# FFN first parts: two of the four pair copies of groups 0 to 6 made by VectorE instead of ScalarE

## The reference

```
xn = layernorm(x)
z = layernorm(xn) * ln1_g + ln1_b
q, v = z @ wq.T + bq, z @ wv.T + bv ; k = q
attn = softmax(q k.T / 4) @ v, 16 heads ; a = attn @ w_out.T + b_out
h = gelu(xn @ ternary(W1).T + b1)            # (4096, 1024)
f = h @ ternary(W2).T + b2
return x + a + f
```

## Time and profile before

| what | value |
|---|---|
| median of 3 runs | 1436.72 us (1434.46 to 1441.07) |
| profiled execution: time, span | 1435.52 us, 1433.7 us |
| busy share of the span: PE, DVE, ACT, POOL | 97%, 93%, 87%, 8% |
| VectorE share of the chain that ended last | 71% (the maxima of line 839: 68%) |
| first parts on ScalarE (line 1020) | 32, mean 1148 ns |
| second parts on VectorE (line 831) | 32, mean 1282 ns |

### The profile page before, as it was taken

How to read it: one execution, slowest core, us unless ns; L and a number is a source line. 1 busy time by engine, 2 the same in 40 slices (tenths; PEclk the granted TensorE clock), 3 DMA queues, 4 the chain that set the end, 5 groups by cost and what they waited for, 6 DMA issues and landing times.

```text
span 1433.7 us, 32248 instructions
## 1 busy us (share of the span) xinstructions
PE 1384.6 (97%) x13414; PEld 447.5 (31%) x13414; DVE 1339.1 (93%) x1430; ACT 1247.3 (87%) x2284; POOL 113.7 (8%) x246
## 2 busy tenths in 40 slices
PE   7899987999999999999999999999999999999999
PEld 5666542222222222222222222222222222222244
DVE  7868779999999999999999999999999999999934
ACT  5554643999999999999999999899999999999975
POOL 2000005000000000000000000000222200002200
PEclk8999999999999999999999999999999999999999
DMA  6012000010000000100000001001212101001122
GB/s 232 16 36 76 30 16 1 28 31 30 31 31 31 30 31 30 31 30 26 29 30 29 32 29 33 28 32 35 60 61 61 61 31 33 32 33 60 39 100 81
DMA packets 28531, 60.69 MB, mean 42 GB/s; under 512 B 6200, under 2 KB 11736, under 8 KB 28130
## 3 DMA queue, kind: packets, MB, share of 16 engines
q1 hardware_dynamic: 27810, 56.99, 11.8%
q10 hardware_dynamic: 576, 1.65, 0.3%
HBM read 41.29 MB, written 16.77 MB: 40 GB/s over the span
## 4 chain that ended last, share of the span: by engine, by line
DVE 71%; PE 23%; ACT 2%; DMA 2%; issue 1%; POOL 0%; SPq 0%; ACTq 0%; DVEq 0%
DVE part_max L839 68%; PE ps L367 6%; PE ps L384 3%; PE ps L1070 3%; PE ps L1139 3%; PE ps L330 2%; PE ps L1085 2%; PE ps L458 1%; DVE w L831 1%; ACT w L1020 1%; DMA rows<-in_rows 1%; PE ps L439 1%; ACT hidden L1015 1%; PE ps L1111 1%; ACT w L1049 1%
## 5 line engine op out<-in xcount | busy, mean ns | idle before, releaser
L1049 ACT ACTIVATE w<-ps 128x512 f32<-128x512 f32 x2048 | 1111.4, 596 | 63.8 <-PE ps L384 21.6
L839 DVE TENSOR_REDUCE part_max<-ps 128x1 f32<-128x1024 f32 x1024 | 1164.8, 1211 | 1.9 <-PE ps L330 1.7
L367 PE MATMUL ps<-w,v_ones 128*32 128x256 f32 (+1 forms) x7688 | 628.6, 399 | 0.4
L384 PE MATMUL ps<-qry,key 50*128 50x512 f16 x1984 | 411.4, 388 | 7.2 <-ACT w L1049 7.0
L330 PE MATMUL ps<-qry,key 48*128 48x512 f16 x2048 | 404.2, 380 | 11.4 <-DVE part_max L839 11.3
L367 PEld LDWEIGHTS ps<-w,v_ones 128*32 128x32 f32 x7688 | 152.2, 108 | 384.7 <-issue 211.5
L384 PEld LDWEIGHTS ps<-qry,key 50*128 50x128 f16 x1984 | 101.1, 93 | 440.7 <-ACT w L1049 412.5
L330 PEld LDWEIGHTS ps<-qry,key 48*128 48x128 f16 x2048 | 101.5, 95 | 36.8 <-DVE part_max L839 26.4
L638 POOL COPY v_ones<-v_all 128x128 f32<-128x128 f32 x64 | 18.6, 291 | 743.9 <-PE ps L367 743.9
L1011 ACT ACTIVATE q_split<-ps,sigma_bq 128x512 f16<-128x512 f32 x16 | 11.0, 687 | 65.2 <-PE ps L1085 65.2
L1070 PE MATMUL ps<-w_ternary,w 128*128 128x256 f16 x512 | 61.7, 277 | 6.2 <-DVE w L831 6.2
(11 more groups left out here) (144 smaller groups left out, 466.2 us busy)
## 6 DMA issues: line engine op xcount, KB each, us to landing
key<-q_parts SPq DMA_DIRECT2D x64, 128.0 KB
qry<-q_parts SPq DMA_DIRECT2D x64, 128.0 KB
o_heads<-o_evacuated SPq DMA_DIRECT2D x31, 256.0 KB, 10.2
resid<-in_x SPq DMA_DIRECT2D x8, 512.0 KB, 13.8
q_parts<-q_split SPq DMA_DIRECT2D x16, 256.0 KB, 2.5
key<-q_parts SPq DMA_DIRECT2D x64, 64.0 KB
qry<-q_parts SPq DMA_DIRECT2D x64, 64.0 KB
out<-resid SPq DMA_DIRECT2D x7, 512.0 KB, 3.1
```

What stands on the lines that cost most here:

```text
L367: mm = eng.matmul(pv[32 * c:32 * c + 2 * D, c0:c1], vst[:, kb, :], prob[kb % 2][:, c * BANK + c0:c * BANK + c1], start=(kb == 0), stop=(kb ...
L384: eng.matmul(ring_bank(v, i, False), key[v][r:r + KROWS, kb * P:(kb + 1) * P], qry[v][r:r + KROWS, c * BANK:(c + 1) * BANK], start=True, s ...
L839: dve.tensor_reduce(part_max[h % 2][:, a // 2, a % 2:a % 2 + 1], pa[a % 2], AX.X, ALU.max).then_inc(s_r, 1)
L1049: act.activation(prob[kb % 2][:, c * BANK:(c + 1) * BANK], ring_bank(k, i, last), ACT.Exp, scale=exp_scale).then_inc(s_e, 1)
```

## The change

In groups 0 to 6 the first parts of pairs 1 and 3 are written by VectorE, with a tensor_scalar (`hidden` times the scale, float16 out) right ahead of the second part of the same pair. It waits for the gelu of the pair's second block, and the second part waits for it through a new semaphore. ScalarE keeps pairs 0 and 2 of these groups and all four of group 7; its counter's values are counted anew. 14 instructions move, none is added in number. TensorE's stream is the same.

```diff
--- before.py
+++ after.py
@@ -266,6 +266,7 @@
         s_h = sem("hidden_psum")
         s_g = sem("gelu_done")
         s_h1 = sem("hidden_part1")
+        s_hd = sem("hidden_part1_dve")
         s_h2 = sem("hidden_part2")
         s_f = sem("ffn_psum")
         s_ra = sem("resid_ffn_added")
@@ -310,6 +311,20 @@
 
 
         BETWEEN = (1, 3, 5)
+
+        def on_dve(g, i):
+
+            return g < NG - 1 and i % 2 == 1
+
+        ACT_PAIRS = [[i for i in range(KF // 2) if not on_dve(g, i)] for g in range(NG)]
+
+        def act_parts(g, i):
+
+            return sum(len(a) for a in ACT_PAIRS[:g]) + sum(1 for n in ACT_PAIRS[g] if n <= i)
+
+        def dve_parts(g, i):
+
+            return KF // 2 * g + i + 1 - act_parts(g, i)
         EARLY = 6
 
 
@@ -825,7 +840,13 @@
                         rows(2 if g == NG - 1 else 1)
                     if i == KF // 2 - 1:
                         value(g, 0)
-                    dve.wait_ge(s_h1, KF // 2 * g + i + 1)
+                    if on_dve(g, i):
+                        dve.wait_ge(s_g, KF * g + 2 * i + 2)
+                        dve.tensor_scalar(hp[0][:, 2 * i:2 * i + 2, :], hid[:, 2 * i:2 * i + 2, :], hs[:, 0:1], None,
+                                          ALU.mult).then_inc(s_hd, 1)
+                        dve.wait_ge(s_hd, dve_parts(g, i))
+                    else:
+                        dve.wait_ge(s_h1, act_parts(g, i))
                     if g == 0 and i == 0:
                         dve.wait_ge(s_wd, 8)
                     dve.scalar_tensor_tensor(out=hp[1][:, 2 * i:2 * i + 2, :], in0=hid[:, 2 * i:2 * i + 2, :],
@@ -1013,7 +1034,7 @@
                 for f in range(KF):
                     act.wait_ge(s_h, KF * g + f + 1)
                     act.activation(hid[:, f, :], pf[f % 2], ACT.Gelu, scale=1.0 / XS, bias=b1_col[:, f:f + 1]).then_inc(s_g, 1)
-                    if f % 2:
+                    if f % 2 and not on_dve(g, f // 2):
                         if first and f == 1:
                             act.wait_ge(s_wd, 4)
                         act.wait_ge(s_g, KF * g + f + 1)
```

## The result

The changed kernel takes 1440.15 us (median of 12 runs, 1437.78 to 1442.92) against 1435.19 us before (12 runs, 1433.56 to 1441.07). The ratio is 1.0025 with a 95% interval of 1.0014 to 1.0037, which is 3.6 us (2.0 to 5.3) at 1436 us. The two medians lie 4.96 us apart, the two means 3.8; I go by the ratio. The forecast was 1439.3 us.

The account below looks back on a forecast made before the run. The chain of waits bounds the kernel, VectorE's last second part setting FFN groups 1 to 3. 1.56 + 0.75 + 0 + 0.3 = +2.6 us on a 1436.72 us median gave 1439.3 us; 8 in 10 within 1435.3 to 1443.2.

Parts of the forecast that it names:

- The copy's cost: Each moved copy on VectorE takes 0.75 us, 0.78 us with the start of the second part behind it.
- The rival at 1.28 us: The copy runs at the two-input operation's rate, 1.28 us: +6.4 us in all, 1443.1 us; chance 0.07.
- Group 0: VectorE is late there without idle time, so both copies are fully paid: 2 x 0.78 = +1.56 us.
- Groups 1 to 3: Pair 3's copy waits behind the value add, so the last second part comes 0.25 us later per group: +0.75 us.
- Groups 4 to 6: Copies hide in VectorE's waits while TensorE's transposes wait 2.35 us for the third maximum: 0 us.
- cover 0.17: In group 4, VectorE is free at 130.11 us, before pair 2's second part at 130.28: 0.17 us to spare.
- The clock: TensorE's longer stand in group 0, 4.5 us, lengthens the low-clock stretch behind it: +0.3 us; group 7's fall unchanged.
- the sum: All terms together: 1.56 + 0.75 + 0 + 0.3 = +2.6 us.
- The one in which the clock pays the loss back: Low-clock stretches at group 0's restart and group 7's transposes both vanish: -0.7 us, 1436.0 us; chance 0.17.
- The relief that pays: Without ScalarE's copy, TensorE's 0.7 us wait in groups 1 to 3 goes: -0.2 us in all, 1436.5 us; chance 0.05.
- The broken cover: Groups 4 to 6 lose 0.2 us each and the clock falls once more: +4.9 us, 1441.6 us; chance 0.14.

Follow-up runs that it names:

- experiment 1: VectorE makes the copies of pairs 1 and 3 in groups 1 to 6 only, group 0 as before; ratio 1.0006 to the kernel before.
- experiment 2: VectorE makes the copies of pairs 1 and 3 in group 0 only; ratio 1.0022 to the kernel before.
- Experiment 3: Kernel before, with ScalarE making all first parts and VectorE also copying pairs 1 and 3 of groups 0 to 6 into an unread spare tile; ratio 1.0026.
- experiment 4: Kernel before, but nobody copies pairs 1 and 3 in groups 0 to 6; GpSimd zeroes these first parts once; ratio 1.0003.
- experiment 5: Against the kernel before, VectorE copies only pair 3 of groups 1 to 3, with half of v's add moved behind the next group's statistics; ratio 0.9999.
- experiment 8: Kernel before, all copies on ScalarE, half of v's add moved later in groups 0 to 3, group 0's five out-scale scalars behind the second parts; ratio 0.9996.
- experiment 6: Changed kernel with pair 1's copy made twice in groups 4 to 6; ratio 1.0038 to the kernel before.
- experiment 11: Changed kernel with the third maximum moved ahead of pair 2's second part in groups 4 to 6; ratio 0.9993 to the kernel before.

## Why the prediction was right

**The copy's cost** (0.75 us, 0.78 with the follower's start) held: 745 ns, and 39.31 to 40.09 is 0.78. The rival at 1.28 us is out. So are the 594 ns that the prediction worked out from the Trainium skill's "VectorE: DVE Perf Modes", section "The TRN2 errata"; that section itself says that its row comes out too short. The interpolation between two rows of the same operation was off by 7 ns.

**Group 0** (+1.56) held: 1.57 us in the trace, and experiments 1 and 2 put the bulk of the loss there. Experiment 3, in which ScalarE keeps its copies, has the same stand: VectorE's time is what counts.

**Groups 1 to 3** (+0.25 each) held: 22.30 us from down products to down products instead of 22.05. The step behind it, that pair 2's second part does not move when pair 1's copy leaves ScalarE, is experiment 4's, where all of the relief shows as 0.53 us behind the v add. Experiments 5 and 8 show the reason, the v add ahead of the copy.

**Groups 4 to 6** (0, cover 0.17) held: 0.16 us in the trace, the stand unchanged, and 0.61 us more of it with a second copy (experiment 6).

**The clock** (+0.3) held in the two profiled executions: the 64 products took 8.79 us against 8.48, and the first maximum of group 4 is 2.57 us late where the sum says 2.6. As a mean over executions it is likely too small. I took one execution each of two lengths of stand. Over the traces a stand of 2.93 us costs 0.86 us on average and one of 4.51 us 2.04, which makes the term about +1.2 and the sum 2.3 + 1.2 = 3.5 us, and 3.6 was measured. The granted clock of all runs says 0.9 us, from 0.1 to 1.7. Neither proves it: the first rests on five traces a class, and the measured interval (2.0 to 5.3) holds the forecast's 2.6 as well as 3.5.

**Luck.** The forecast of 1439.3 us is only 0.9 us under the measured median because two errors partly cancel. It started from a median of 1436.72 us over three runs, 1.5 above that of twelve, and its change of 2.6 us is 2.4 under the distance of the two medians (1.0 under the ratio's 3.6).

**The rivals.** The one in which the clock pays the loss back needed both low stretches to go. In group 0 the low stretch never went after the longer stand, in five traces; ahead of group 7 it did go in the profiled execution, but one came in group 6.

The relief that pays: refuted by experiments 3 and 4, except that experiment 5 shows where it would be true. The broken cover: not seen in the changed kernel, and shown in experiments 6 and 11 to be 0.17 us from it. I had left out how much that free place depends on the order of the maxima, since it does not enter this forecast; in experiment 11 the copies of groups 4 to 6 cost three times 1.2 us.

## What to carry to other kernels

Price a moved instruction at its new place in the new engine's row: what stands ahead of it and whether that engine is itself late there, not which engine is busier. Work that hides in another engine's stand is free only as long as the stand is, so look for the reason of the stand first; here one maximum moved ahead of one second part in three groups was worth 8.9 us, where the moved copies cost 3.6. A stand of TensorE can also have a price behind it, because of the clock: add it as a mean over several traces, not from one.

## What the runs showed of the hardware

- A tensor_scalar on VectorE from float32 in SBUF runs at the same rate with float16 out as with float32: 745 ns for 1024 elements a partition with float16 out, where the line between 351 ns (256) and 1286 ns (2048) with float32 out gives 752. The instruction with two tensor inputs takes 1284 ns.
- GpSimd's two MEMSETs of 128x1024 (1.83 us together) held one tensor_scalar of 128x256 on VectorE that began 0.15 us after them: it took 1.83 us instead of 0.40 (experiment 4).
- After a stand of 4.51 us the low clock (0.50) lasted 3.4 us in three executions and 6.8 in two; after one of 1.44 us it did not come in four; after 2.93 us it came in three of five. At the start of the heads, between 223 and 257 us, one low stretch was 6.8 us long in seven executions, 10.2 in six and 13.7 in one, and three of the fourteen had another of 3.4 us shortly before it. Of the seven with 6.8 us, six had a further 3.4 us that began between 917 and 929 us, and no other execution had one there. So in the heads, up to the stretch at the very end, the clock was low for 10.2 us in eleven of the fourteen and for 13.7 in three. In the two executions compared above, 3.4 us more of it cost 1.27 us and gave back 1.22. I found nothing in the kernels that goes with these lengths; that stays open.
